# Layer 0 attention: value products in pairs of steps, both fills behind the second scores, three probability buffers

## The reference, cut to what matters

```python
q = rms_norm(x @ q_kernel); k = rms_norm(x @ k_kernel); v = x @ v_kernel   # 16 heads of q, 4 of k and v, 16 wide
q, k = rope(q), rope(k)
probs = softmax(q @ k.T / 4)            # no mask, per sequence and head: 512 x 512
x = layernorm(x + (probs @ v) @ out_kernel)
x = layernorm(x + shared_expert(x) + top1_of_8_experts(x * sigmoid(logit)))
x = layernorm(x + causal_attention_16_heads(x))
x = layernorm(x + ffn_4bit_with_lora(x))
```

## Time and profile before

| | us |
|---|---|
| median of 3 runs (853.47 to 854.2) | 854.17 |
| span of the profiled execution, first to last instruction | 851.4 |
| what lies around the span, by the median | 2.8 |
| TensorE busy | 767.9 |
| DVE busy | 446.6 |
| ScalarE busy | 359.7 |
| GpSimd busy | 115.4 |

### The profile page before, as it was taken

One profiled execution on the slowest core, in us unless ns is written; L12 is line 12 of the kernel. 1 busy time (PEld: TensorE's weight loads), 2 busy tenths in 40 slices (PEclk: granted clock), 3 DMA queues, 4 the chain that ended last, 5 costly groups with the idle time before them and its releaser, 6 DMA issues. The chain is left out here.

```text
span 851.4 us, 11512 instructions
## 1 busy us (share of the span) xinstructions
PE 767.9 (90%) x3907; PEld 409.4 (48%) x3908; DVE 446.6 (52%) x1198; ACT 359.7 (42%) x565; POOL 115.4 (14%) x127
## 2 busy tenths in 40 slices
PE   5599999999999999999997879888998989989886
PEld 3222444444435556666665445434464445533675
DVE  2744554565435622222247676868765674662453
ACT  3389775685684012212223233444423442156030
POOL 0000000000000311111842411231011110022000
PEclk9699999999999999999999899989999999999999
DMA  7567207005107161111125870006300370000000
GB/s 217 148 204 223 93 26 209 27 25 149 38 26 247 43 198 46 43 45 46 32 84 169 251 201 2 1 27 187 110 1 3 106 216 1 2 1 26 14 12 26
DMA packets 51582, 75.01 MB, mean 88 GB/s; under 512 B 7607, under 2 KB 44763, under 8 KB 49227
## 3 DMA queue, kind: packets, MB, share of 16 engines
q1 hardware_dynamic: 49660, 69.26, 27.0%
q0 software_dynamic: 1872, 5.11, 2.2%
HBM read 46.57 MB, written 27.66 MB: 87 GB/s over the span
## 5 line engine op out<-in xcount | busy, mean ns | idle before, releaser
L656 PE MATMUL ps<-arena 128*128 128x256 f32 (+3 forms) x1084 | 326.7, 450 | 18.2 <-issue 2.9
L656 PEld LDWEIGHTS ps<-arena 128*128 128x128 f32 x1084 | 201.2, 195 | 106.6 <-issue 68.7
L970 ACT ACTIVATE arena<-ps 128x1024 f32<-128x1024 f32 x128 | 124.2, 1027 | 32.9 <-PE ps L711 32.6
L1067 ACT ACTIVATE arena<-ps 128x1024 f32<-128x1024 f32 (+3 forms) x128 | 82.9, 702 | 114.1 <-PE ps L903 114.0
L1450 DVE TENSOR_REDUCE arena<-ps 128x1 f32<-128x512 f32 (+3 forms) x176 | 100.4, 633 | 28.5 <-PE ps L881 27.6
L769 PE MATMUL ps<-arena 128*128 x184 | 86.5, 593 | 0.6 <-DVE arena L1177 0.6
L711 PE MATMUL ps<-arena 96*128 96x512 bf16 x256 | 71.4, 390 | 7.0 <-DMA arena<-q_stacks_dram 3.9
L1565 POOL TENSOR_SCALAR_AFFINE_SELECT arena<-arena 128x512 f32<-128x512 f32 x64 | 41.7, 652 | 253.3 <-ACT arena L1067 253.3
L725 PE MATMUL ps<-arena 128*32 128x512 f32 x512 | 69.6, 611 | 2.9 <-DVE arena L1223 2.7
L879 PE MATMUL ps<-arena 96*128 96x128 bf16 (+3 forms) x256 | 62.3, 303 | 9.6 <-DVE arena L1450 5.7
L648 PE MATMUL ps<-arena 128*128 128x128 f32 (+3 forms) x237 | 38.6, 302 | 23.3 <-DVE arena L1216 10.5
(11 more groups left out here) (153 smaller groups left out, 678.4 us busy)
## 6 DMA issues: line engine op xcount, KB each, us to landing
arena<-stacks_dram SPq DMA_DIRECT2D x16, 768.0 KB, 5.9
arena<-in_gate_up_proj SPq DMA_DIRECT2D x8, 1024.0 KB, 9.3
arena<-q_stacks_dram SPq DMA_DIRECT2D x8, 768.0 KB, 5.8
stacks_dram<-arena SPq DMA_DIRECT2D x16, 384.0 KB, 3.3
arena<-in_down_proj SPq DMA_DIRECT2D x8, 512.0 KB, 8.7
stacks_dram<-arena SPq DMA_DIRECT2D x16, 256.0 KB, 3.3
q_stacks_dram<-arena SPq DMA_DIRECT2D x8, 384.0 KB, 4.1
yg_dram<-arena SPq DMA_DIRECT2D x23, 128.0 KB, 1.7
```

The source lines that it names most:

```text
L656: last = nc.tensor.matmul(dst[0:rows, lo:hi], a, w, start=(n == 0), stop=(n == len(pairs) - 1))
L970: nc.scalar.activation(probs[:, 2 * p:2 * p + 2, :], ps[:, 2 * p:2 * p + 2, :], ACT.Exp)\
L1067: nc.scalar.activation(cprobs[:, i % 2, 2 * p:2 * p + 2, P * kt:S], ps[:, 2 * p:2 * p + 2, P * kt:S], ACT.Exp).then_inc(exp_done[p], 1)
```

## The change

The list of stage A is written by a new function. For two steps k and k+1 (k even) it has: S(k+2), P(k), P(k+1), S(k+3), F(k), F(k+1). Before, the same work stood as S(k+1), F(k), P(k), S(k+2), F(k+1), P(k+1). ScalarE's order becomes E(k+2), the copy of L977 if P(k+1) ends a group, E(k+3), and then what both fills need. The probabilities go through three buffers in place of two, so that E(k) waits for P(k-3); the third lies in the memory of `gate_up` of expert 6, whose load moves from behind `layer0_stacks(2)` to the end of the attention, beside expert 7's. Stage C and the strings of fills are unchanged.

```diff
+def paired_order(fills, name):
+
+    n = NT * HG
+    steps = [(name + "S", 0, 0), (name + "S", 0, 1)]
+
+    def scores(k):
+        if k < B * n:
+            steps.append((name + "S", k // n, k % n))
+
+    for b, fill in enumerate(fills):
+        *fill, rest = fill.split("|")
+        assert len(fill) == n and not rest.strip()
+        for i in range(0, n, 2):
+            k = b * n + i
+            scores(k + 2)
+            steps += [(name + "P", b, i), (name + "P", b, i + 1)]
+            scores(k + 3)
+            steps += expand(fill[i] + " " + fill[i + 1], b, [0])
+    return steps
...
-    return (expand(A_START, 0, [0]) + attention_order([A_FIRST, A_SECOND, A_THIRD, A_LAST], "att")
+    return (expand(A_START, 0, [0]) + paired_order([A_FIRST, A_SECOND, A_THIRD, A_LAST], "att")
...
-        probs1 = gu[:, E - 1, :, :].rearrange("p c (a n) -> p (c a) n", a=2)
+        probs1, probs2 = (gu[:, e, :, :].rearrange("p c (a n) -> p (c a) n", a=2) for e in (E - 1, E - 2))
...
+        def probs_of(k):
+            return (probs0, probs1, probs2)[k % 3]
...
             layer0_stacks(2)
-            gate_up_load((6,))
             xs_store(1)
...
             sp.wait_ge(pv_done, head0 * B)
-            gate_up_load((7,))
+            gate_up_load((6, 7))
...
-                                                (probs0, probs1)[i % 2][:, g, :], start=(kt == 0), stop=(kt == NT - 1))
+                                                probs_of(k)[:, g, :], start=(kt == 0), stop=(kt == NT - 1))
...
-                    if head0 * b + i >= 2:
+                    if head0 * b + i >= 3:
 
-                        act.wait_ge(pv_done, head0 * b + i - 1)
-                    probs = (probs0, probs1)[i % 2]
+                        act.wait_ge(pv_done, head0 * b + i - 2)
+                    probs = probs_of(head0 * b + i)
```

## The result

The changed kernel takes 879.77 us, the median of 4 runs (876.99 to 883.04), against 854.18 before in the same comparison: 1.0289 times as long, 95% interval 1.0262 to 1.0317. That is 25.6 us more by the medians and 24.7 by the ratio. I had said 872, slower, in a range of 860 to 880.

The account below looks back on a forecast made before the run. TensorE was taken to bound the attention nearly throughout. The order's -4.7 us and 22.0 of new waits gave +17.3, or 18.4 with roundings carried; +18 was taken, for 872.2 us, range 860 to 880.

Parts of the forecast that it names:

- the walk: Pairs of the attention in order, each new wait added: 22.0 us of waits, +18 in all, 872.2 us; chance 0.56.
- The order alone: The 30 pairs from S(3) to S(63): without new waits, S(63) would start 4.7 us earlier.
- light pair: Pair with fill under about 1.4 us, leaving E(k+3) uncovered: 5.07 us, against 4.65 before; 14 of 30 pairs.
- R behind N: F(22) and F(23): R needs both copies of N from ScalarE; wait 1.9 us.
- Q behind X: F(32) and F(33): Q needs the copies of X from ScalarE; wait 1.95 us.
- ScalarE held by R: R on ScalarE waits for the DVE behind the rope, delaying E(26); S(27) waits 3.8 us, its second half 0.5.
- Table loads at E(28) and E(44): Same table load ahead of each, now covered by two P instead of a fill and a P: 0.7 and 0.8 us.
- The stacks: S(32) waits 3.65 us for the stack of sequence 2; sequence 3 the same, 1.4 us.
- V0 behind D1: P(32) needs V0 on the DVE, behind F3 and D1's sum: wait 2.5 us; P(16) 0.35, P(48) 0.25.
- T2's copy: F(42), F(43): it holds ScalarE until T0's parts are in DRAM; S(47) and its second half wait 2.45 us, Su1 1.35.
- The third buffer and expert 6's load: Buffer costs no instruction; the load, moved behind the attention, costs nothing, about 3 us if its cover were gone.
- the clock as a rival: TensorE's clock halves for 5.5 us after idling at S(27) and S(32): at most 5.5 us more, 877.7; chance 0.18.

Follow-up runs that it names:

- The light pairs' share: Only the eight light pairs of sequence 0 in the new order, all others in the old one; 856.86 us, ratio 1.0042 to the kernel before.
- the run with TensorE kept at work: Changed kernel with 12 and 4 repeated score products ahead of the stack waits of sequences 2 and 3; 878.57 us, ratio 1.0289.
- the run with R early: Changed kernel with the N transposes moved to F(20) and R to F(22), the rope behind R; 873.09 us, ratio 1.0221.
- the run with V0 first: Changed kernel with V0 ahead of F3 in the strings of sequences 1 and 2; 874.11 us, ratio 1.024.
- the run of the old order: Changed kernel with stage A back in the old order, three buffers and the later load of expert 6 kept; 853.47 us, ratio 0.999.
- hybrids: Kernels with some pairs in the new order and others in the old: light pairs old 877.56 us, eight dependent pairs old 868.96, only eight full pairs new 866.66.
- the eight full pairs: Only eight full pairs without dependence inside the pair in the new order, all the rest in the old one; 866.66 us, ratio 1.0139.
- the light pairs old: Changed kernel with the 16 pairs of little fill in the old order, all others paired; 877.56 us, ratio 1.0266.
- the last run: Old order with V0 ahead of F3, and P beside P at six places with the fills left apart; 851.41 us, ratio 0.9981.

## Why the prediction was right

The direction and the mechanism came out: nearly all that was lost is idle time of TensorE, at the places that the walk named. The size was short, +18.0 us said and +25.6 measured, and the time lies 0.2 us inside the end of the range, with two of its four runs beyond it. That it fell inside is in part luck.

- *The order alone.* 5.07 a light pair was 5.09, and 3.51 + fills was 3.50 where it was read. The light pairs' share was then run by itself. But the 4.7 us are not a gain of the pairs. By these rows 14 light pairs lose 6.2 (0.44 each) and 16 full ones gain 3.7, so the order by itself costs 2.5. The walk comes to -4.7 because it also leaves out the waits that before itself had, 1.23 at P(16), 1.44 at P(32), 0.63 ahead of T0 and smaller ones, 5.5 in all; V0's come back among the 22.0. No run shows the order with a gain.
- *R behind N*: 1.9 said, 1.81 in after. *Q behind X*: 1.95 said, 1.81.
- *ScalarE held by R*: S(27) at 123.15 said, 124.09 measured. The wait before it was 2.30 and not 3.8, since R, S(26) and P(24) ran slow at the low clock: S(26) took 1.91. Here the low clock cost almost nothing, as it ate into a wait; in the run with TensorE kept at work it had not fallen there, and the wait was 3.93. That the rope held R is shown by the run with R early, where R waits 0.77 for the DVE in place of 5.98; its N moved too, but ScalarE's wait was for the DVE in both.
- *Table loads at E(28) and E(44)*: 0.7 and 0.8 said, 0.5 and 0.5 measured, at S(29) and S(45).
- *The stacks*: 3.65 said for S(32), 3.56 measured; 1.4 for S(48), 0.94 measured, with Su2 and Su3 slow before it. No run took the wait away; one only filled it.
- *V0 behind D1*: 2.5 said, 2.36 measured, and shown by the run with V0 first.
- *T2's copy*: S(47) at 219.0 said, 224.81 measured, a lag of 5.8 that all comes from before it. Its waits, 1.91 and 0.31, and Su1's, 1.72, add to 3.9 as against 3.8. This one is read from the trace; no run took it away.
- *The third buffer and expert 6's load*: nothing, as said, by the run of the old order.

What was off is one term. I had the clock as a rival with a chance of 0.18 and 5.5 us, and kept it out of the sum. It came true. My walk gives S(63) at 271.8 and it was 278.89. The 7.1 us between can be read from the rows. S(3) came 1.2 late, with P(0) and P(1) still at the low level (2.91); in the run of the old order S(3) stood at 49.24 as well, so that part need not be the order's. From S(32) to S(34) it was 13.65 where it is 10.6 at the high level, 3.0 more, and from P(32) to S(35) 3.32 for 1.86, 1.5 more. Su2 and Su3 took 5.12 for 3.6, 1.5 more. That makes 7.2.

So the forecast of 872 was the sum without the clock, and the measured 879.8 is a little above the rival's 877.7. The rival's figure came out for other places than it named. It had 2.75 at S(27) and at S(32); at S(27) the clock cost almost nothing, and 3.0 of the loss was at P(32), Su2 and Su3, which it did not name. My argument against it was that an idle time of 1.44 us had cost nothing. That says little of an idle time of 3.65. In which of the places the clock falls changes from one run to the next, and with it the time. Before's own executions beside the first hybrids ran from 851.6 us at a mean granted clock of 0.972 to 859.6 at 0.961.

My figures for the hybrids were wrong three times. I added up pairs and didn't look at the seam between them; how much of each miss is the seams' and how much the clock's was split only for the eight full pairs.

## What to carry to other kernels

In a software pipeline written out by hand, the thing to ask of each reorder is not how often an engine switches but what covers each dependent operation: pairing two products left two scores side by side, and the exponentials between them bare. Work that is put back to back must not depend on itself through another engine; walk each engine's queue in its own order, and price a copy together with what is already queued before it. And an idle time on TensorE has a second price, the half-speed stretch that may stand behind it: here each of over 3 us had one, and of those between 2.3 and 2.8 us about half.

## What the runs showed of the hardware

- TensorE's clock fell to its low level behind every idle time of over 3 us seen between S(3) and S(63) (3.56 in after; 3.54, 3.53, 3.37, 3.24 at S(32) and 3.93 at S(27) in other runs). With products in the gap at S(32) it stayed up, and 3.0 us came back. "TensorE: Matmul & The Clock Gate" of the Trainium skill, Why this matters for your kernels, warns of idle gaps over about 3 us between bursts of matmuls; the trace agrees.
- Shorter gaps go either way. Behind the same 2.36 us at P(32) the clock fell in after and in the run with TensorE kept at work (P and P took 3.39 and 3.47), and stayed up with R early and with the light pairs old (1.92). At S(48) it fell behind 2.61 and 2.77 us, and not behind 2.37 and 2.57. Two waits in a row, 1.72 at Su1 and 1.9 at S(47), were followed by a fall at Su2 in three of the six traces that have them. One of 1.44 us never brought it down. In the last run it fell with no idle time at all, behind the router's product.
- Two P in a row take 1.86 us to the next S and one takes 1.00, so a float32 product into four column groups costs 0.86 us when another of the same follows.
- ScalarE started E(26) at 123.01 us, as the table load from 121.72 ended. The drain of 1.38 us that "ScalarE: Activation LUTs" of the Trainium skill, What ACT_TABLE_LOAD costs, adds to a switch is not seen behind the load here, nor was it before.
